# Where a kernel adds up its weight blocks: in SBUF on GpSimd for every round, or in DRAM by accumulating transfers once per layer

## What is computed

```python
q, k, v = x @ Wq, x @ Wk, x @ Wv
attn_out = softmax(q @ k.T * 512**-0.5) @ v @ Wp + bp
cms_out  = gelu(attn_out @ cW1 + cb1) @ cW2 + cb2 + one_hot(code)      # 512 -> 2048 -> 512
modifier = gelu(concat([attn_out, cms_out]) @ mW1 + mb1) @ mW2 + mb2   # 1024 -> 2048 -> 512
y = clip(x + cms_out + modifier, 0, 1)
u = gelu(y @ W_down[role] + b_down[role]) @ W_up[role] + b_up[role]    # adapter, 512 -> 256 -> 512
x = layernorm(y + u) * gamma[role] + beta[role]
```

## Time and profile before

| | |
|---|---|
| median of three runs | 2156.77 us |
| the profiled execution's own time | 2156.44 us |
| its span in the trace | 2154.8 us |
| TensorE busy | 2105.6 us (98%) |
| VectorE busy | 1537.7 us (71%) |
| ScalarE busy | 1042.1 us (48%) |
| GpSimd busy | 598.7 us (28%) |
| DMA, mean rate | 68 GB/s |

### The profile page before, as it was taken

How to read it: one execution, slowest core, us unless ns; L and a number is a source line. 1 busy time by engine, 2 the same in 40 slices (tenths; PEclk the granted TensorE clock), 3 DMA queues, 4 the chain that set the end, 5 groups by cost and what they waited for, 6 DMA issues and landing times.

```text
span 2154.8 us, 24846 instructions
## 1 busy us (share of the span) xinstructions
PE 2105.6 (98%) x9256; PEld 1724.7 (80%) x9256; DVE 1537.7 (71%) x1923; ACT 1042.1 (48%) x1527; POOL 598.7 (28%) x620
## 2 busy tenths in 40 slices
PE   8999999999999999999999999999999999999997
PEld 6888887888788887888877888788887888878884
DVE  4366678776867668876776766977686866787676
ACT  5264445454446444544554544444454644454444
POOL 1001136452001113655000111655400011355420
PEclk9999999999999999999999999999999999999999
DMA  8101131212202112221312111321130211311211
GB/s 304 40 10 59 59 88 49 59 48 78 100 20 88 59 59 69 59 59 59 116 41 88 40 59 42 96 59 59 40 127 20 102 46 59 88 50 59 59 59 39
DMA packets 125767, 146.41 MB, mean 68 GB/s; under 512 B 5952, under 2 KB 100160, under 8 KB 123728
## 3 DMA queue, kind: packets, MB, share of 16 engines
q1 hardware_dynamic: 122912, 130.05, 18.9%
q0 software_dynamic: 1504, 8.49, 1.9%
q10 hardware_dynamic: 1232, 6.29, 0.7%
HBM read 123.84 MB, written 12.58 MB: 63 GB/s over the span
## 4 chain that ended last, share of the span: by engine, by line
PE 85%; DVE 10%; ACT 2%; issue 2%; DMA 0%; SPq 0%; ACTq 0%; DVEq 0%
PE bank L615 28%; PE bank L617 28%; PE bank L616 28%; DVE ring L1321 2%; DVE vc L1363 2%; DVE pc L1493 1%; DVE xa L1358 1%; DVE lsum L1695 1%; ACT ring L955 1%; ACT raw L1098 0%; PE bank L923 0%; DVE xs L1700 0%; DVE xs L1653 0%; DVE xs L1685 0%; DVE raw L1439 0%
## 5 line engine op out<-in xcount | busy, mean ns | idle before, releaser
L1321 DVE TENSOR_TENSOR ring<-stage,ring 128x1024 fp32r<-128x1024 f32 (+1 forms) x312 | 363.4, 1176 | 103.8 <-ACT ring L955 103.6
L551 POOL TENSOR_TENSOR stage<-stage 128x256 f32<-128x256 f32 x120 | 106.3, 886 | 1122.1 <-DMA stage<-cms_w 904.5
L615 PE MATMUL bank<-ph_hi,ring 128*128 128x512 f32 x1048 | 410.6, 392 | 5.4 <-issue 2.4
L617 PE MATMUL bank<-ph_hi,ring 128*128 128x512 f32 x1048 | 407.9, 389 | 0.0
L616 PE MATMUL bank<-ph_lo,ring 128*128 128x512 f32 x1048 | 407.9, 389 | 0.0
L615 PE MATMUL bank<-xa,ring 128*128 128x512 f32 x1016 | 396.0, 390 | 2.9 <-DVE xs L1653 2.1
L617 PE MATMUL bank<-xa,ring 128*128 128x512 f32 x1016 | 395.3, 389 | 0.0
L616 PE MATMUL bank<-xa,ring 128*128 128x512 f32 x1016 | 395.3, 389 | 0.0
L955 ACT ACTIVATE ring<-stage 128x1024 fp32r<-128x1024 f32 (+1 forms) x312 | 296.3, 970 | 111.7 <-PE bank L617 78.3
L615 PEld LDWEIGHTS bank<-ph_hi,ring 128*128 128x128 f32 x1048 | 196.7, 188 | 53.7 <-issue 7.2
L617 PEld LDWEIGHTS bank<-ph_hi,ring 128*128 128x128 f32 x1048 | 196.7, 188 | 41.0
(11 more groups left out here) (159 smaller groups left out, 3139.6 us busy)
## 6 DMA issues: line engine op xcount, KB each, us to landing
stage<-mod_w SPq DMA_DIRECT2D x128, 256.0 KB, 3.4
stage<-cms_w SPq DMA_DIRECT2D x36, 512.0 KB, 3.6
stage<-mod_w SPq DMA_DIRECT2D x32, 512.0 KB, 4.9
stage<-cms_w SPq DMA_DIRECT2D x56, 256.0 KB, 4.3
fold_staging<-fold_w SPq DMA_DIRECT2D x16, 512.0 KB, 5.2
stage<-folded SPq DMA_DIRECT2D x16, 512.0 KB, 4.3
xs<-pc POOLq DMA_DIRECT2D x8, 1024.0 KB, 8.3
stage<-ada_w SPq DMA_DIRECT2D x16, 512.0 KB, 3.6
```

The costliest lines, as they stand in the source:

```text
L551: pool.tensor_tensor(part(S1), part(S2), part(A22), ALU.add).then_inc(sums_ready, 1)
L615: pe.matmul(dst, lh, rh, start=start and n == 0, stop=False, skip_group_check=not start)
L617: done = pe.matmul(dst, ll, rh, start=False, stop=n == last, skip_group_check=not start)
L1321: dve.tensor_tensor(ring_part(key, 1), staged(key), f32(ring_part(key, 0)), ALU.subtract).then_inc(w_lo, 1)
```

## The change

A DRAM tensor `ready_w` holds, for each of the 2 layers and 30 pieces, all seven blocks (7 x 128 KB). A load brings the seven blocks with one transfer of 896 KB (`load_ready`), and ScalarE's split waits for that transfer alone. The seven blocks are made in two steps. SyncE copies source blocks to the seven places, DRAM to DRAM (`prepare`: seven transfers of 128 KB for A or C; three of 256 KB and one of 128 KB for D). GpSimd then issues accumulating transfers, DRAM to DRAM, of 128 KB as 16 rows of 8 KB: three per piece (`sum_once`), and, one slot later, two per piece (`sum_twice`). Layer 0 is made ready at the start and in round 0, layer 1 in round 1; in rounds 2 and 3 nothing is made. The pieces go in batches: in round 0, 2 and 3 pieces before slot 1, then 2 per slot to slot 7 and 3 per slot after; in round 1, 2 per slot, then 4. SyncE copies batch n at its slot n + 1, GpSimd adds at its slots n + 2 and n + 3. The plain down projections are loaded as before. GpSimd's adds in SBUF are gone. `UP_AT` and `DOWN_AT` reorder the blocks; group sizes stay.

```diff
-UP_AT = {A11: 0, A12: 1, S1: 2, S2: 3, A22: 4, S3: 5, S4: 6}
-DOWN_AT = {A11: 0, S2: 1, S1: 2, A12: 3, A22: 4, S3: 5, S4: 6}
+UP_AT = {A11: 0, A12: 1, S1: 2, S2: 3, S3: 4, A22: 5, S4: 6}
+DOWN_AT = {A11: 0, S1: 1, S2: 2, A12: 3, S3: 4, A22: 5, S4: 6}
...
+EARLY = (2, 3)
+BATCHES_READY, READY_IN = {}, {}
+for prep_layer in range(LAYERS):
+    prep_left = list(PIECES_READY)
+    for prep_n in range(-len(EARLY) if prep_layer == 0 else 0, SLOTS):
+        prep_size = EARLY[prep_n] if prep_n < 0 else 2 if prep_n < CH else 3 + prep_layer
...
+    ready_w = nc.dram_tensor("ready_w", (LAYERS, len(PIECE_AT), STAGE_BLOCKS, P, BLK), F32, kind="Internal").ap()
...
+        def batch_in(r, n):
+
+            layer = 0 if r == 0 else r // 2 + 1 if r % 2 else LAYERS
+            return layer if BATCHES_READY.get((layer, n)) else None
...
+            def load_ready(key):
+
+                layer, at = key[0] // 2, STAGE_OF[key]
+                to = stage[at]
+                n = READY_IN[layer, key[1:]]
+                sp.wait_ge(w_lo, STAGE_FREE[key])
+                sp.wait_ge(prepared[n], 16 * batch_count(layer, n, lambda kind: 2))
+                sp.dma_start(to[:, :, :], ready_piece(layer, *key[1:]).rearrange("b p n -> p b n")).then_inc(stage_in[at], 16)
+
+            def prepare(layer, slot):
...
+                        halves = piece.rearrange("p (k m n) -> p k m n", k=4, m=2)
+                        for block, m, k in under:
+                            sp.dma_start(to[UP_AT[block], :, :].rearrange("p (k n) -> p k n", k=2),
+                                         halves[:, 2 * k:2 * k + 2, m, :]).then_inc(copied[slot], 16)
...
             for r in range(ROUNDS):
                 load((r, "P"), cms_w[2 * (r // 2) * CH, :, :])
+                if r == 0:
+                    sp.wait_ge(fold_out[1], 16 * LAYERS)
+                    prepare(0, -2)
                 load_up(r, 1)
+                if r == 0:
+                    prepare(0, -1)
                 load_down(r, 0)
...
                 for n in range(1, SLOTS):
+                    if batch_in(r, n - 1) is not None:
+                        prepare(batch_in(r, n - 1), n - 1)
                     if n + 1 < SLOTS:
                         load_up(r, n + 1)
...
-                pool.wait_ge(stage_in[STAGE_OF[key]], 16 * STAGE_NTH[key])
-                pool.tensor_tensor(part(S1), part(S2), part(A22), ALU.add).then_inc(sums_ready, 1)
-                pool.tensor_tensor(part(S3), part(S2), part(A11), ALU.add).then_inc(sums_ready, 1)
...
+            def sum_once(layer, slot):
+
+                pool.wait_ge(copied[slot], 16 * batch_count(layer, slot, COPIES.get))
+                for kind, n in BATCHES_READY[layer, slot]:
+                    w, at = ready_piece(layer, kind, n), UP_AT if kind in ("A", "C") else DOWN_AT
+                    for block, more in ((S1, A22), (S3, A11), (S4, A22)):
+                        pool.dma_start(rows(w, at[block]), rows(w, at[more]), accum_op=ALU.add, max_dma_last_dim=8192).then_inc(summed_once[slot], 16)
+
+            def sum_twice(layer, slot):
+
+                pool.wait_ge(summed_once[slot], 16 * batch_count(layer, slot, lambda kind: 3))
...
+                    for block in (S2, S4):
+                        pool.dma_start(rows(w, at[block]), rows(w, at[S3]), accum_op=ALU.add, max_dma_last_dim=8192).then_inc(prepared[slot], 16)
...
+                for n in range(CH, SLOTS):
                     if n > CH:
                         hidden_sum(r, n - 1, T4)
-                    sums((r, "A", n + 1))
-                    if n == CH:
+                    else:
                         residual(r, 1)
-                        sums((r, "C", n + 1))
-                    sums((r, "D", n))
-                    if n > CH:
-                        sums((r, "C", n + 1))
-                    hidden_sum(r, n, T1)
-                    hidden_sum(r, n, T3)
-                    hidden_sum(r, n, T2)
-                hidden_sum(r, SLOTS - 2, T4)
+                    sum_ahead(r, n)
+                    if n < SLOTS - 1:
+                        hidden_sum(r, n, T1)
+                        hidden_sum(r, n, T3)
+                        hidden_sum(r, n, T2)
...
             def split_hi(key):
 
                 piece = key[:3]
-                if len(key) == 4:
-                    act.wait_ge(sums_ready, SUM_AT[piece] + (3 if key[3] == 0 else 4))
-                else:
-                    act.wait_ge(stage_in[STAGE_OF[piece]], 16 * STAGE_NTH[piece])
+                act.wait_ge(stage_in[STAGE_OF[piece]], 16 * STAGE_NTH[piece])
```

More of the change, by code:

```diff
@@ L223, with batch_count @@
     stage_held[stage_at].append(piece_key)
[L225 to L234, removed]
+PIECES_READY = []
+for prep_n in range(1, SLOTS):
+    PIECES_READY.append(("A", prep_n))
+    if prep_n >= CH:
+        PIECES_READY.append(("C", prep_n))
+        if seven(prep_n - 1):
+            PIECES_READY.append(("D", prep_n - 1))
+PIECE_AT = {piece: n for n, piece in enumerate(p for p in PIECES_READY if p[0] != "E")}
+COPIES = {"A": 7, "C": 7, "D": 4, "E": 7}
+EARLY = (2, 3)
[4 more added lines that the diff above has]
+        prep_size = EARLY[prep_n] if prep_n < 0 else 2 if prep_n < CH else 3 + prep_layer
+        BATCHES_READY[prep_layer, prep_n], prep_left = prep_left[:prep_size], prep_left[prep_size:]
+        for piece in BATCHES_READY[prep_layer, prep_n]:
+            READY_IN[prep_layer, piece] = prep_n
+def batch_count(layer, n, per_piece):
+    return sum(per_piece(kind) for before in range(layer + 1) for kind, _ in BATCHES_READY.get((before, n), ()))
 PLAIN_RING = {"P": 4, "A0": 0, "A1": 4, "U0": 8, "U1": 14, "d0": 0, "d1": 4, "u0": 8, "u1": 14}
@@ L294, in build @@
         stage_in = [sem(f"stage_in{n}") for n in range(3)]
-        sums_ready, w_hi, w_lo = sem("sums_ready"), sem("w_hi"), sem("w_lo")
+        w_hi, w_lo = sem("w_hi"), sem("w_lo")
+        copied, summed_once, prepared = ({n: sem(f"{name}{n + len(EARLY)}") for n in range(-len(EARLY), SLOTS - 1)}
+                                         for name in ("copied", "summed_once", "prepared"))
         fold_in = [sem(f"fold_in{i}") for i in range(4)]
@@ L438, in load @@
                 at = STAGE_OF[key]
-                runs = stage[at][:, 0:6, :].rearrange("p (g b) n -> p g (b n)", g=2)[:, :, 0:2 * BLK]
                 sp.wait_ge(w_lo, STAGE_FREE[key])
[L441 to L446, removed]
-                else:
-                    sp.dma_start(stage[at][:, 0:4, :].rearrange("p k n -> p (k n)"), src).then_inc(stage_in[at], 16)
+                sp.dma_start(stage[at][:, 0:4, :].rearrange("p k n -> p (k n)"), src).then_inc(stage_in[at], 16)
@@ L457, in load_up @@
             def load_up(r, n, part="A"):
[L458 to L462, removed]
+                load_ready((r, part, n))
             def load_down(r, n):
@@ L467, in load_down @@
                     load((r, "D", n), cms_w[2 * (layer * CH + n) + 1, :, :])
+                elif seven(n):
+                    load_ready((r, "D", n))
                 else:
@@ L541, in _, with rows, sum_ahead @@
                                   avecs[bass.ds(role + ROLES * layer, 1), :, :].rearrange("a p n -> (a p) n")).then_inc(avec_in, 16)
[L543 to L548, removed]
-                pool.wait_ge(stage_in[STAGE_OF[key]], 16 * STAGE_NTH[key])
-                pool.tensor_tensor(part(S1), part(S2), part(A22), ALU.add).then_inc(sums_ready, 1)
-                pool.tensor_tensor(part(S3), part(S2), part(A11), ALU.add).then_inc(sums_ready, 1)
[L553 to L556, removed]
+            def rows(w, block):
+                return w[block, :, :].rearrange("(g q) n -> g (q n)", q=2048 // w.shape[2])
+            def sum_once(layer, slot):
+                pool.wait_ge(copied[slot], 16 * batch_count(layer, slot, COPIES.get))
+                for kind, n in BATCHES_READY[layer, slot]:
+                    w, at = ready_piece(layer, kind, n), UP_AT if kind in ("A", "C") else DOWN_AT
[3 more added lines that the diff above has]
+                pool.wait_ge(summed_once[slot], 16 * batch_count(layer, slot, lambda kind: 3))
+                for kind, n in BATCHES_READY[layer, slot]:
+                    w, at = ready_piece(layer, kind, n), UP_AT if kind in ("A", "C") else DOWN_AT
+                    for block in (S2, S4):
+                        pool.dma_start(rows(w, at[block]), rows(w, at[S3]), accum_op=ALU.add, max_dma_last_dim=8192).then_inc(prepared[slot], 16)
+            def sum_ahead(r, n):
+                for step, before in ((sum_twice, 3), (sum_once, 2)):
+                    if n >= before and batch_in(r, n - before) is not None:
+                        step(batch_in(r, n - before), n - before)
             def hidden_sum(r, n, blk):
```

33 lines of the change are left out of this document (27 added, 6 removed).

## The result

The changed kernel takes **2170.94 us** (median of four runs, 2168.78 to 2173.88) against 2157.88 of the kernel before, run beside it (2155.68 to 2159.92). The ratio is 1.0062, with a 95% interval of 1.0044 to 1.0079: slower, by more than the 0.2% that a measurement tells from no change. The forecast was 2144 with a range to 2158, and the other sign.

What follows compares the result with a forecast made beforehand. TensorE, 98% busy, was taken as the bound with a floor of 2089 us, winnable only where it waits around slot 8. 2156.44 - 13.5 + 1.0 = 2143.9, given as 2144 us; own range 2139 to 2150, full range to 2158.

Steps and rivals of the forecast that it cites:

- POOL's adds go: Around slot 8: without POOL's adds VectorE comes free 2.9 to 4.2 us sooner per round; 13.5 us gained in all.
- Loads grow. Cost 0: Piece loads: 896 KB instead of 512 lands in 5.0 us, ready sooner than before with adds; cost 0.
- the residual bounds slot 8: Slot 8 rival: three larger loads hold back both residual transfers, the gain is only 3 us, 2154 us; chance 0.07.
- SyncE's copies: SyncE's queue, rounds 0 and 1: 8.5 us of copy issues ahead of the next A's load stay hidden, later slots just.
- its 2178 us: Cms slots, by the skill's 0.95 us per copy: each 2.4 us late, 14 slots 34 us, time 2178 us.
- DMA engines: Rounds 0 and 1: copies, accumulating transfers and larger loads add 217 us per 520 us round, some 60% busy.
- In all I charge 1 us: Rounds 0 and 1: total charge of 1 us; POOL's issues make T1 between 0 and 1.2 us late, twice.
- The mild case: Some eight slots of rounds 0 and 1: 0.87 us issues and late C load give back 8 to 12 us; chance 0.10.
- crowded queue: Cms slots: copies ahead of the next A make TensorE wait from 0.78 us per copy; 2186 to 2233 us; chance 0.09.
- POOL holds the hidden sums: Rounds 0 and 1: waiting accumulating issues delay the hidden sums, 150 us or more; chance 0.04.
- the three signs: Seven operations staying at 1.7 us; TensorE waiting in cms slots, rounds 0 and 1; ScalarE waiting for DMA, rounds 2 and 3.
- the other test that it named: Sign of hidden copies: the same count of matmuls in rounds 0 and 1 as in 2 and 3.

Runs made afterwards that it cites:

- D8's load: Changed kernel without copies and accumulating transfers, the load of D8 asked for only after the second residual transfer has landed: 2139.97 us, ratio 0.9918.
- The version at 2141.43: Changed kernel with 3 pieces per slot for both layers, late load of D8, and sums of slots 9 to 15 issued after T2: 2141.43 us, 0.9922.
- 2152.86: Changed kernel with 3 pieces per slot for both layers and D8 loaded after the second residual transfer, sums not moved: 2152.86 us, 0.9975.
- one wait: Kernel before, with GpSimd's adds of C9 and D8 in slot 8 held back until VectorE's last step in `cms_end`: 2145.57 us, 0.9942.

## Why the prediction was wrong

The account by medians: 2158.9, adds gone -18.9, larger loads +6.1, copies +0.1, GpSimd's issues +0.7, the accumulating transfers' bytes +24.0, makes 2170.9. The medians of the kernel before differ by half a us between the groups (by 1.1 us with the first one, 2157.88), and by the ratios two steps between groups come out otherwise: GpSimd's issues 3.5 us instead of 0.7, D8's load 3.7 instead of 6.2. So a step is good to about 3 us: the adds and the bytes stand clear of that, the copies and the issues can't be told from 0. The traces bear the bytes out: between the wait of 0.6 us that ends slot 8 and the one of 0.70 us behind slot 15, the kernel after loses 24.2 us in rounds 0 and 1 against the kernel without copies and sums, and 1.5 us in slot 8 of the four rounds.

*"POOL's adds go": right in mechanism, mis-sized.* The term for slot 8 was 13.5 and the traces show 13.8. A second site at the round ends added 2.7; I had looked at VectorE only in slot 8. Of the 12 adds only the eight of C9 and D8 fall into the 12.73 us of the seven operations, A9's four lie before them; so holding back those eight alone could give most of it. The prices held: beside GpSimd's issues of transfers, where its adds had been, the first of the seven operations takes 1.22 us and the last one 1.23 (timelines of VectorE and ScalarE, kernel after):

```profile
316.62 1.22 DVE L1680 SCALAR_TENSOR_TENSOR raw<-raw,pc 128x1024 f32<-128x1024 f32 x1
...
327.76 1.23 DVE L1430 TENSOR_TENSOR vc<-raw,vc 128x1024 fp32r<-128x1024 f32 x1 [4.01 <-ACT vc L1048]
```

```profile
326.67 1.06 ACT L1048 ACTIVATE vc<-raw 128x1024 fp32r<-128x1024 f32 x1 [4.85 <-DMA xs<-pc]
```

The Trainium skill (SBUF — State Buffer, section Who interferes with whom) says that a VectorE instruction with two SBUF inputs contends with a GpSimd instruction that reads SBUF. The traces agree: 1.6 to 2.65 us beside the adds, 1.22 without.

*"Loads grow. Cost 0": wrong.* I asked whether the larger load is there in time for its split, and it is. I didn't carry through what else it delays, although "the residual bounds slot 8" was on the list, at 0.07. In round 0 VectorE was to come free at 327.2. The second residual transfer landed 10.5 us after its issue instead of 8.3 (the median of all eight is 11.0), ScalarE waited 4.85 us for it, and VectorE's last low part ended at 328.99. TensorE still lost 1.42 us to a low part at 334.08, nearly the old 1.52. That rival's mechanism, a larger load that holds back the residual, cost 6.1 us in four rounds.

*"SyncE's copies": right.* Estimated 0.41 us of engine time, 0.1 us of time in all. The engines' share rose by 20.3 points of 150 us (53.3 less 33.0) for 9.28 MB, some 0.43 us per 128 KB, and a load landed 0.1 us later. The warning of the Trainium skill (DMA: Bandwidth & Descriptors, section Bandwidth) against small transfers, from which the prediction had its 2178 us, did not come true for these copies.

*"DMA engines": the occupancy was right and the conclusion wrong; this step failed.* An accumulating transfer was to take 0.64 us of engine time. Queue 0 was busy 35.8% of 150 us for 78 of them: 0.69 us. The share was to be "some 60%" in rounds 0 and 1 and 27% after; it was 67%, 65% and 28% (rounds 0, 1 and 2), but 71% and 83% in the 150 us behind slot 8. The round's mean hid that the work isn't even. Above all the step treated busy engines as free so long as they weren't full, and kept 5.0 us for a load. Beside the accumulating transfers it takes 9.6 us in the median and up to 19.9. A C load in these slots has some 10.3 us by the reading above and took up to 14.8; I had only worked out the slack of A.

*"In all I charge 1 us": wrong by the factor of 24.* The mild case had the right place, a late C load, with 8 to 12 us, and the wrong cause: GpSimd's issues. It takes 1.0 us per issue, above my 0.61 to 0.87, and by the medians this costs 0.7 us in all.

*What the sums' cost hangs on.* The version at 2141.43 has engines busier (88%) and loads slower (10.0 us) than the change itself, and TensorE waits for none. So neither occupancy nor the median landing decides, but which load meets the transfers, and how much slack it has. It is the C load, issued late in a slot beside the batch between T4 and T1. Three things show it: all four stalls of round 1 stand behind C loads of over 10 us; with the batch moved, these land in 5.1 to 6.3 us, and the time falls by 11.4 us (2152.86 to 2141.43); and loads of A and D that take longer cost nothing in either kernel. Why a load slows so much more beside these transfers than beside the copies, whether by their 8 KB rows, the accumulating, or two queues taking turns, no run here separates. Accumulating transfers without the copies weren't tried. The Trainium skill (DMA: Bandwidth & Descriptors, section Issuing engines are not separate DMA queues) says that transfers run on the same 16 DMA engines whoever issues them, and interleave. The traces agree: GpSimd's bytes delayed SyncE's loads from 5.4 to 9.6 us.

The rivals "crowded queue" and "POOL holds the hidden sums" in its strong form both fell: TensorE has no wait in slots 2 to 7 of rounds 0 and 1. Of the three signs by which the prediction was to be known as wrong, the first two did not come, and of the third only two waits of ScalarE of 0.9 us, which TensorE didn't feel. What told was the other test that it named, equal counts of matmuls in all rounds: 637 and 583 against 664.

## What to carry to other kernels

Work that is moved to the DMA engines is not free because they are less than full: for each load near it, compare its landing time under that traffic (here two to almost four times the quiet one) with its own slack, and place the batches where they meet the loads that have slack. When an engine's work goes, look through the whole round for where it slowed another engine, not only at the largest stall, and before rebuilding it try to move it: one wait gave three quarters of the best gain.

## What the hardware showed that I had not expected

Behind three of the four stalls of round 1 TensorE's granted clock fell. In four us behind the stall at 919.93 (the stretch, and two matmuls of the timeline):

```profile
921.00:925.00 4.00, 4.00 (x13) 3.14 (x12) 4.00 (x5) 2.70 (x5) 1.94 (x1) 0.63 0.88 248
...
921.69 0.63 PE L687 MATMUL bank<-xa,ring 128*128 128x512 f32 x1
922.12 0.63 PE L685 MATMUL bank<-vc,ring 128*128 128x512 f32 x1
```

The granted clock is 0.63 in the mean, with some matmuls at the lower level (1.2 GHz): seven start 0.43 us apart instead of 0.226, which adds 1.4 us to the stall. It happened behind the stalls of 3.08, 4.45 and 2.50 us, and not behind the one of 2.29 us, so some 4 of the 24 us are the clock's (an estimate, three times 1.4).

A DRAM to DRAM copy of 128 KB from SyncE lands in 3.6 to 3.8 us, and an accumulating one in 5.7, or 7.6 in the crowded slots.
